# A three-layer interaction kernel: a wider buffer for the direct sums, one more split pair in each tile, and another order of pairs on TensorE

## What is computed

```python
x0 = xk = e                                  # (B, 39, 16)
for W, b in ((w0, b0), (w1, b1), (w2, b2)):  # W: (39, k, 128), k = 39, 64, 64
    z = relu(einsum('bhd,bkd,hks->bsd', x0, xk, W) + b[None, :, None])
    # layers 0 and 1: the first 64 units are the next xk, the last 64 are "direct"
    # layer 2: all 128 units are direct
logit = concat(direct, axis=1).sum(axis=-1)  # (B, 256): the sum over the 16 dims
h = relu([logit, dense_ctx] @ W_top1 + b_top1)
y = relu(h @ W_top2 + b_top2) @ W_top3
```

## Time and profile before

| | |
|---|---|
| median of 3 runs | 1373.23 us (1372.33 to 1373.45) |
| the profiled execution | 1374.53 us, of which 1372.70 us from the first instruction to the last (the span) |
| granted clock of TensorE, mean over the span | 0.994 |
| matmul records, 32 tiles and the tower | 4142 |

### The profile page before, as it was taken

The page is one execution under the profiler, slowest core; times in us unless marked ns, Lnnn a source line. Parts: engine busy times, 40 slices in busy tenths (PEclk is TensorE's granted clock), DMA queues, the critical chain, the costliest instruction groups (busy, mean ns, idle before and its releaser), DMA issues.

```text
span 1372.7 us, 15527 instructions
## 1 busy us (share of the span) xinstructions
PE 1249.4 (91%) x4142; PEld 770.8 (56%) x4142; DVE 1166.7 (85%) x1057; ACT 655.3 (48%) x758; POOL 907.7 (66%) x581
## 2 busy tenths in 40 slices
PE   0189999997999999999999999999999999999989
PEld 0045565565665656665665566665655666665643
DVE  1259999997999999999999999999999999999850
ACT  1135554544545454455545454455545454454532
POOL 6648877766777777676777777676777744555520
PEclk9999999998999999999999999999999999999999
DMA  7199777778877777788877777788877777678500
GB/s 178 16 235 229 169 157 188 176 194 167 201 156 161 187 182 194 176 199 206 199 161 165 189 173 194 179 195 206 199 170 154 193 177 191 176 196 193 124 0 0
DMA packets 133861, 233.49 MB, mean 170 GB/s; under 512 B 15891, under 2 KB 23044, under 8 KB 133730
## 3 DMA queue, kind: packets, MB, share of 16 engines
q1 hardware_dynamic: 80333, 146.77, 45.9%
q10 hardware_dynamic: 43522, 83.90, 23.3%
q0 software_dynamic: 9984, 2.58, 2.6%
HBM read 229.33 MB, written 6.23 MB: 172 GB/s over the span
## 4 chain that ended last, share of the span: by engine, by line
PE 41%; POOL 20%; DVE 19%; issue 15%; ACT 3%; DMA 1%; DVEq 1%; ACTq 0%; POOLq 0%
PE z_even L742 18%; PE z_odd L742 14%; POOL gathered L418 13%; DVE whole L634 9%; POOL rest L430 7%; DVE rest L641 4%; DVE whole_psum L634 4%; ACT head L519 2%; PE z_even L749 2%; PE z_odd L749 2%; PE whole_psum L822 2%; DVE part L669 2%; PE x_odd L769 1%; PE x_odd L822 1%; PE x_even L822 1%
## 5 line engine op out<-in xcount | busy, mean ns | idle before, releaser
L430 POOL TENSOR_TENSOR rest<-whole,head 128x1024 fp32r<-128x1024 f32 x256 | 609.3, 2394 | 310.5 <-ACT head L519 298.6
L634 DVE TENSOR_TENSOR whole<-x_banks,x_rep 128x1024 f32<-128x1024 f32 x448 | 535.2, 1216 | 57.7 <-ACT x_banks L494 57.0
L418 POOL DMA_INDIRECT gathered<-in_tbl,idx x312 | 296.5, 950 | 102.8 <-issue 100.1
L519 ACT CAST head<-whole_psum 128x1024 fp32r<-128x1024 f32 x192 | 194.8, 1014 | 347.9 <-DVE whole_psum L634 295.6
L519 ACT CAST head<-whole 128x1024 fp32r<-128x1024 f32 x256 | 269.0, 1051 | 47.7 <-DVE whole L634 20.1
L641 DVE TENSOR_TENSOR rest<-whole_psum,head 128x1024 fp32r<-128x1024 f32 x192 | 234.6, 1222 | 22.1 <-ACT head L519 21.9
L634 DVE TENSOR_TENSOR whole_psum<-x_banks,x_rep 128x1024 f32<-128x1024 f32 x192 | 235.6, 1227 | 10.3 <-DMA x_rep<-x_rows 7.8
L742 PE MATMUL z_odd<-head,w_rest 128*128 128x512 f32 x460 | 205.2, 446 | 25.1 <-POOL rest L430 19.1
L742 PE MATMUL z_even<-head,w_rest 128*128 128x512 f32 x436 | 194.1, 445 | 24.8 <-issue 10.8
L742 PE MATMUL z_odd<-whole,w_whole 128*128 128x512 f32 x400 | 188.5, 601 | 5.5 <-DVE whole L634 5.5
L742 PE MATMUL z_odd<-rest,w_head 128*128 128x512 f32 x460 | 180.2, 392 | 0.0
(11 more groups left out here) (76 smaller groups left out, 890.3 us busy)
## 6 DMA issues: line engine op xcount, KB each, us to landing
x_rep<-x_rows SPq DMA_DIRECT2D x160, 512.0 KB, 10.2
x_rep<-x_rows ACTq DMA_DIRECT2D x160, 512.0 KB, 10.5
x_shift<-x_rows SPq DMA_DIRECT2D x93, 546.0 KB
gathered<-in_tbl,idx POOLq DMA_INDIRECT x312
x_rows<-xt SPq DMA_DIRECT2D x32, 78.0 KB
x_rows<-xt SPq DMA_DIRECT2D x32, 40.0 KB
x_rep<-in_W_top SPq DMA_DIRECT2D x2, 512.0 KB, 11.8
w_k<-in_L_rec_w SPq DMA_DIRECT2D x1, 760.5 KB
```

What stands on the lines that cost most here:

```text
L418: nc.gpsimd.indirect_dma_start(gathered[:, f, :], None, tables[f], bass.IndirectOffsetOnAxis(ap=idx[:, f:f + 1], axis=0)).then_inc(s_gathe ...
L430: nc.gpsimd.tensor_tensor(rest[:, split_slot(product)], whole_slot(product), head[:, split_slot(product)].bitcast(F32), ALU.subtract).then ...
L519: nc.scalar.copy(head[:, split_slot(product)], src).then_inc(s_head, 1)
L634: nc.vector.tensor_tensor(out[0:rows, 0:width, :], xk[0:rows, :].unsqueeze(1).to_broadcast([rows, width, N]), x0, ALU.mult).then_inc(s_pro ...
```

## The change

The diff has three parts, cut here to their core; the lists of loads, semaphores and a few index functions follow from them.

**Direct sums.** TOGETHER becomes 4 (a whole block), direct01 and direct2 become [sample, dim] in the columns, ACT's relu writes each dim's 128 samples 64 bytes apart, and DVE adds once a block, over 16 dims that lie side by side. part and its addition go. The reduce of layer 2 now stands in front of layer 2 of the next block's first tile, the one of layers 0 and 1 after pair 3 of layer 2 of each block's last tile. The relu of layer 2 moves on ACT behind all heads of the next tile's layer 1. ctx_t moves into partitions 64 to 79 beside xt, and its weights with it.

**Kinds.** Whole pairs of layer 2 go from 4 to 3, so split pairs of a tile go from 14 to 15: nine rests on the Pool (4 in layer 1, 5 in layer 2) and six on DVE (4 and 2). A rest of kind V comes one pair after its product (DEFER = 1) instead of two. The gathers are spread: five behind the last rest of layer 1, three between rests of layer 2, and what is left of a tile's 10, 10, 11 or 8 at the end of layer 2.

**Order on PE.** PE takes pair 4 of layer 1 (whole) ahead of 2 and 3, and in layer 2 pair 4 ahead of 2 and 3, and 7 ahead of 5 and 6. The transposes come after one pair of layer 1.

```diff
-KINDS = {1: "UVPPUPVPVP", 0: "UUUU", 2: "UUVUPUVPVP"}
+KINDS = {1: "UVPVUPVPVP", 0: "UUUU", 2: "UPVPUPPUVP"}
+SPLITS = {layer: len(kinds) - kinds.count("U") for layer, kinds in KINDS.items()}
+PE_ORDER = {1: (0, 1, 4, 2, 3, 5, 6, 7, 8, 9), 2: (0, 1, 4, 2, 3, 7, 5, 6, 8, 9)}
-GATHERS_BETWEEN = 11
-HEADS_IN_1 = 3
-HEADS_IN_2 = 1
-TRANSPOSES_AFTER = 2
-ADD_2_AFTER = 4
-ADD_01_AFTER = 1
-DEFER = 2
+GATHERS_AFTER = {1: (0, 0, 0, 5), 2: (1, 1, 0, 1, 0)}
+GATHERS_OF_TILE = (10, 10, 11, 8)
+D2_AFTER = 8
+XT_AFTER = 3
+X1_AFTER = 3
+TRANSPOSES_AFTER = 1
+ADD_01_AFTER = 3
+DEFER = 1
-TOGETHER = 2
+TOGETHER = TPB
+D0_AFTER = 4
...
-        direct01 = sb("direct01", [P, TOGETHER, N])
-        direct2 = sb("direct2", [P, TOGETHER, N])
-        part = sb("part", [P, P])
+        direct01 = sb("direct01", [P, P, DIM])
+        direct2 = sb("direct2", [P, P, DIM])
...
+            def relu_by_sample(direct, t, z_rows, b):
+                d = t.first % TPB * DPT
+                return relu(direct[:, :, d:d + DPT].rearrange("p b d -> p d b"),
+                            z_rows.rearrange("p (d b) -> p d b", d=DPT), b)
...
+                for n in range(SPLITS[1] + 1):
+                    if n == D2_AFTER and (t.turn is not None or t.first > 0):
+                        out_layer2(t.plus(-1))
+                    if n == XT_AFTER and has_transposes(t):
+                        transposed(t)
+                    heads(t, 1, start=n, upto=n + 1, loads={1: [0], 2: [1]} if has_layer0(t) else {})
+                out_layer1(t)
+                for n in range(SPLITS[2] + 1):
+                    if n == X1_AFTER and has_layer0(t):
+                        next_x1(t)
+                    if n == D0_AFTER and has_layer0(t):
+                        next_direct(t)
+                    heads(t, 2, start=n, upto=n + 1, loads={5: [2], 8: [3], 9: [4]} if has_layer0(t) else {})
...
-            def add_dims(out, direct, t, done, partial):
+            def add_dims(out, direct, t, done):
...
+                nc.vector.tensor_reduce(cols, direct[:], AX_X, ALU.add).then_inc(done, 1)
...
-                    layer12(t, 1, x1_bank, {ADD_2_AFTER: lambda: add_layer2(t.plus(-1))} if ends else {})
+                    layer12(t, 1, x1_bank, {})
...
                 if has_layers12(t):
+                    if t.first % TOGETHER == 0 and (t.turn is not None or t.first > 0):
+                        add_layer2(t.plus(-1))
                     dve.wait_ge(s_x2, t.count(2, 2))
```

More of the change, by code:

```diff
@@ L264, in wait_used @@
         def wait_used(eng, product):
-            eng.wait_ge(s_used, before(*product) + 1)
+            t, layer, j = product
+            place = j if layer == 0 else PE_ORDER[layer].index(j)
+            eng.wait_ge(s_used, before(t, layer, 0) + place + 1)
         def wait_rest(eng, product):
@@ L274, in split_slot, with ring_place, before_in_place @@
             return number(*product, "PV") % SPLIT_SLOTS
+        in_period = TPB * sum(kind in "UP" for kinds in KINDS.values() for kind in kinds)
+        def ring_place(product):
+            return number(*product, "UP") % in_period % WHOLE_SLOTS
+        place_of = {(step, layer, j): ring_place((Tile(step), layer, j)) for step, layer, j in run_order
+                    if KINDS[layer][j] in "UP"}
+        def before_in_place(t, layer, j):
+            now = run_order.index((t.first, layer, j))
+            found = [x for x in run_order[:now] if place_of.get(x) == place_of[t.first, layer, j]]
+            if not found:
+                return None
+            step, layer, j = found[-1]
+            return Tile(step, t.turn), layer, j
         def whole_slot(product):
-            return whole[:, number(*product, "UP") % WHOLE_SLOTS]
+            return whole[:, ring_place(product)]
         def stage(t, layer):
@@ L432, in rests @@
                                             ALU.subtract).then_inc(s_rest_p, 1)
[L433 to L436, removed]
+                    for _ in range(GATHERS_AFTER[layer][n] if refill is None else 0):
+                        if fields:
+                            gather(fields.pop(0))
+                while layer == 2 and fields:
+                    gather(fields.pop(0))
             pool.wait_ge(s_ids, 16)
@@ L467, in body @@
                 else:
-                    fields = list(range(k * per_tile, min((k + 1) * per_tile, FIELDS)))
+                    first = sum(GATHERS_OF_TILE[:k])
+                    fields = list(range(first, first + GATHERS_OF_TILE[k]))
                     if k == 0:
@@ L526, in out_layer2 @@
                     wait(act, s_sum2, t.visits(TOGETHER))
-                relu(direct2[:, t.first % TOGETHER, :], z_of(t, 2)[:], bias[:, 2:3]).then_inc(s_d2, 1)
-            def body(t):
[L530 to L545, removed]
+                relu_by_sample(direct2, t, z_of(t, 2)[:], bias[:, 2:3]).then_inc(s_d2, 1)
@@ new lines, in transposed @@
+            def transposed(t):
+                nxt = t.plus(AHEAD)
+                if nxt.first % TPB == 0:
+                    act.wait_ge(s_gather, nxt.blocks(16 * FIELDS, 16 * FIELDS))
+                    wait(act, s_x0, nxt.count(1))
+                    nc.scalar.copy(emb[:], gathered[:].rearrange("p f d -> p (f d)").unsqueeze(1)
+                                   .to_broadcast([P, SPC, FIELDS * DIM])).then_inc(s_emb, 1)
+                act.wait_ge(s_x0, nxt.count(1, 1))
+                wait(act, s_stored, nxt.count(32, -32))
+                nc.scalar.copy(xt[:, nxt.first % 2, :],
+                               x0_bank[nxt.first % 2][0:FIELDS, :]).then_inc(s_xt, 1)
@@ L546, in body @@
+            def body(t):
+                if not has_layers12(t):
+                    if has_transposes(t):
+                        transposed(t)
                     if not has_layer0(t):
                         nc.scalar.copy(x_shift[:, 0, :], x0_bank[0][0:ROWS0, :]).then_inc(s_first, 1)
[L548 to L570, removed]
@@ L627, in product @@
                     out = whole_slot(now)
-                    last = earlier(t, layer, j, "UP", WHOLE_SLOTS)
+                    last = before_in_place(t, layer, j)
                     if last is not None and kind_of(last) == "U":
```

72 lines of the change are left out of this document (42 added, 30 removed).

## The result

The changed kernel takes 1405.15 us (median of four runs, 1403.99 to 1407.27) against 1373.34 for the kernel before: a ratio of 1.0217 [1.019, 1.0243]. It is slower by 2.2%; 1342 and faster was forecast. The profiled execution took 1407.3, of which 1405.4 are span.

The account below looks back on a forecast made before the run. PE's work, DVE's reduces and the Pool at layer 2's start were taken to bound by turns. Gains of 22 (six blocks), 8.7 (tiles 26 to 30) and 1.5 took 1374.5 to 1342; own range 1333 to 1352, wider range 1330 to 1368.

Parts of the forecast that it names:

- 2.3 taken: DVE's 2048-element reduce: 2.3 us assumed, priced like products that read side by side; upper bound 3.9.
- the hop as the price: DVE's reduces: the long 1.95 us per 1024 elements comes from strided reading; were it the operation's, 24 us more.
- The margin of 0.2 in layer 1: Layer 1, pairs 7 and 9: a rest is ready in 3.85 us while PE does three splits in 4.08.
- its bound of 1.1: ACT's strided relu: upper time 1.1 us, scaled from DVE's hopping read; below 0.68; both said to hide.
- dear reduces: Rival: DVE's 2048-element reduces cost 3.9 us, 24 us more in all, giving 1366; chance 0.12.
- the Pool as bound: Rival: the Pool's chain of rests and gathers in layer 2 sets the time, slower at 1390; chance 0.10.
- late loads: Rival: loads land 4 us later, PE loses about 1 us a tile, near 1372, no change; chance 0.08.
- dear relus: Rival: ACT's strided relu at 3 us delays layer 2's first head, 0.5 us a tile, 1357; chance 0.06.
- I allow 0.4: Layer 1 of a block's third tile: 0.4 us for the emb copy standing before transposes that come one pair earlier.
- the 1.6 us which the third tile loses: Layer 1 of a block's third tile in the kernel before: 1.6 us lost, put down to DVE's reduce.
- The first two tiles and the last: about 1.5 together: Edge tiles outside the six blocks and the tail: a gain of about 1.5 us in the sum.
- More of them behind: First two tiles: three gathers, not ten, in front of layer 2's rests, and more gathers behind those rests.

Follow-up runs that it names:

- the run with the sums alone: Kernel before with only the direct sums of the change, ACT's loop moved by 75 instructions: 1362.55 us, ratio 0.9916.
- moved by 75: Changed kernel with 75 one-element copies added on ACT ahead of its loop, so the body stands 75 instructions later: 1381.34 us, ratio 1.0022.
- moved by 16: Kernel before with 16 one-element copies added on ACT ahead of its loop, nothing of the change in it: 1411.21 us, ratio 1.025.
- moved by 40: Changed kernel with 40 one-element copies added on ACT ahead of its loop: 1437.17 us, one run.
- the run without a branch: Changed kernel with ACT's loop written out for all 32 tiles, other engines keeping their loops: 1378.44 us, ratio 1.0008.
- the early gathers in their old places: Changed kernel with the 13 gathers of each of tiles 0 and 1 placed as in the kernel before: 1406.01 us, ratio 1.0195.
- the fastest run: Changed kernel, 75 copies ahead of ACT's loop, gathers 11, 12, 11, 5, PE's transposes and copy of x later in third tiles: 1339.25 us, ratio 0.9731.

## Why the prediction was wrong

**The steps on the engines' work held.** Groups of lines after, beside the earlier trace rows (mean ns):

```profile
L453 POOL TENSOR_TENSOR rest<-whole,head 128x1024 fp32r<-128x1024 f32 x288 | 688.1, 2398 | 273.3 <-ACT head L548 265.1 <-issue 6.5
L707 DVE TENSOR_REDUCE sum<-direct 128x2048 f32 x14 | 31.9, 2276 | 0.0
L517 ACT ACTIVATE direct<-z_odd,bias 128x512 f32<-128x512 f32 x17 | 20.1, 1183 | 6.1 <-PE z_odd L778 6.1
```

The reduce of 2048 took 2276 ns (2.3 taken), 1.11 ns an element against 1.90 before. That agrees with the hop as the price; the sums also became longer (16 elements in place of 8), and no run parts the two. The rests stayed at 2.40. The margin of 0.2 in layer 1 was enough: 15.1. Layer 2 came out at 65.5 a block, and in tiles 26 to 30 at 76.3 together (75.8). The gather that stood still in tile 5 stood 10.26 us, before 9.83. The strided relu took 1.18, just over its bound of 1.1, and hid. DVE waited nowhere for x_rep (before 7.8 us in all). So dear reduces, the Pool as bound, late loads and dear relus were not the cause, though "slower" came true.

**Failed: "I allow 0.4" for the copy of emb.** Without the branch stall it cost 3.9 (19.0 against 15.1): about 1.9 are the wait for the gathers, gone in the run that made them a tile earlier (17.1), and as much again the copy and what stands behind it, gone with the copy moved as well (15.14). The step named the copy and the transposes, but not what the copy waits for. The gathers that the change moved into layer 2 of the tile before land 6.1 us after the last one's end, and behind the copy stand PE's transposes, the copy of x and the next head. Six tiles, 21 us over the forecast.

The kernel before had a sign of it. In its tile 14 PE waits for this copy:

```profile
642.59 1.06 PE L769 MATMUL x_even<-ident,emb 128*117 128x128 f32 x4 [0.68 <-ACT emb L540]
```

The prediction put the 1.6 us which the third tile loses down to the reduce. In the run with the sums alone no reduce is left in that layer, and it still takes 16.4 us in four of the six third tiles, where the layers 1 without the copy and without a reduce take 15.2; PE waits there 0.73 us for the copy. Its tile 14:

```profile
637.97 1.06 PE L770 MATMUL x_even<-ident,emb 128*117 128x128 f32 x4 [0.73 <-ACT emb L550]
```

```profile
633.99:650.35 16.36, 15.63 (x62) 11.15 (x61) 14.52 (x14) 9.24 (x10) 13.14 (x8) 1.00 0.74 219
```

So about 1.1 of the 1.6 us were not the reduce's.

**Failed: "The first two tiles and the last: about 1.5 together", as a gain.** "More of them behind" was seen, and taken as good. Ten gathers that trail layer 2 in tiles 0 and 1 made emb of tile 2 wait 9.91 us. About 11 us lost.

**Left out: where ACT's loop stands.** The sum has no term for reading instructions; ACT's steps of a turn went from 307 records in the trace to 315 and begin a few places later, and each branch now waits 8 us. The cost is 24 to 31 us in the runs that take it away. The Trainium skill, "Runtime: NRT & Kernel Launch", "Instruction fetch mechanics", says this: an engine holds two blocks of 256 instructions, reads ahead in a straight line only, and a taken branch to a block no longer held waits for a read. The trace agrees that the branch waits and that place decides; the reads on q14 are of 8 KB, where the page has blocks of 16. An estimate from that page's figures: a body of 315 fits into two blocks only if it starts at most 197 places behind a block's start, a body of 307 at most 205. An offset of 57 to 70 instructions ahead of the trace's first record, which no view shows and which is fitted here, then sorts the five places that were run: records 135 (before) and 216 (moved by 75) free, 141 (after), 151 (before, moved by 16) and 181 (moved by 40) not. If the second stall of the last one, ten records on, is its block's end, the offset is 65, inside that span; this is only argued. Nor is the size of a block shown: in the run without a branch a packet of 8 KB falls every 128 records of ACT in the mean, and pieces of 128, of which a body may touch three but not four, sort the same five places. That place decides is shown by runs; which rule of place is not.

**The account.** Over the forecast's 1342 the profiled execution has 65 us: 25 at the branch and 21 at the copy of emb in six tiles, 11 in tile 2, 3 until the first layer 1 begins (90.2, before 87.0), 2 in the last layer 2, the rest in tile 1 and in parts under a microsecond. With the first three mended the run took 1339, but 9 us of that are the layer 2 without gathers, so what the forecast's own steps give is about 1348, and that 1339 lies so near 1342 is partly luck. What sets the start (tile 1 begins at 127 to 134 us in these runs, at 138.5 with the early gathers in their old places) and the last layer 2 (19.7 to 22.1) stays open.

## What to carry to other kernels

When a transfer's issue is moved to a later place, follow its landing to the instruction that waits for it, and then what stands behind that one on its engine; a copy of 1.75 us cost 3.9 here. Before a change inside a hardware loop is judged by its time, look at the packets of the instruction queue on the page: if they grow with the turns, the time tells where the loop stands and not what the change is worth. Sixteen copies made while ACT was idle, ahead of its loop, cost the kernel before 2.5%, and 75 gave the changed one nearly 2% back.

## What the runs showed of the hardware

- At a loop's branch behind which q14 carried reads, ACT stood still for 7.9 to 8.5 us (30 branches in five runs). A packet of 8 KB took about 0.5 us; the last one in each of these waits began 6.0 to 6.8 us behind the branch, so most of the wait lies ahead of it. In the run moved by 40 a second wait of 5.8 us followed ten records on.
- ACT writing 512 columns, each 64 bytes behind the last, took 1.16 to 1.18 us against 0.68 in one piece.
- A DVE sum over 16 neighbours took 1.11 ns an element, a sum over 8 elements 512 bytes apart 1.90.
- ACT got a block's rows 5.5 to 6.1 us (once 7.3) after the last gather's instruction on the Pool ended, where it waited for nothing else (the run without a branch).
- The 114th gather stood still for 10.26 us in the changed kernel, 9.83 in the one before and 3.17 in the fastest run. Why is open.
